# A four-layer graph network on one core: the edge stage of layer 0 keeps its sums in PSUM, with the node's own term copied there by ScalarE

## What is computed

```python
m_in = jnp.concatenate([h[src], h[dst], edge_attr], axis=1)
m = relu(m_in @ eW1 + eb1) @ eW2 + eb2
agg = jax.ops.segment_sum(m, dst, num_segments=h.shape[0])
h_upd = _mlp(jnp.concatenate([h, agg], axis=1), nW1, nb1, nW2, nb2)
return _layer_norm(h + h_upd, ln_gamma, ln_beta)
```

## Time and profile before

| | us |
|---|---|
| median of 3 runs | 4426.26 (4425.43 to 4427.96) |
| the profiled execution | 4430.56 |
| its span in the profile | 4428.8 |
| first addition out of PSUM in the stage begins | 615.7 |
| last accumulation of the stage begins | 1436.4 |

### The profile page before, as it was taken

The page is one execution under the profiler, slowest core; times in us unless marked ns, Lnnn a source line. Parts: engine busy times, 40 slices in busy tenths (PEclk is TensorE's granted clock), DMA queues, the critical chain, the costliest instruction groups (busy, mean ns, idle before and its releaser), DMA issues. The chain is left out here.

```text
span 4428.8 us, 52906 instructions
## 1 busy us (share of the span) xinstructions
PE 2686.6 (61%) x11454; PEld 1433.4 (32%) x11454; DVE 3253.1 (73%) x7572; ACT 719.6 (16%) x2122; POOL 2983.3 (67%) x2929
## 2 busy tenths in 40 slices
PE   4244578888887799466666656578888853000007
PEld 4144332222222688233233334344444422000004
DVE  7497458888888233489999976499989986666664
ACT  0011100000000233233333322111111102000004
POOL 0577667777765577677777737677777745777772
PEclk8555799999999899777888878787888876555558
DMA  3235346666665333466666733376666643444441
GB/s 159 36 113 156 76 123 179 178 178 171 175 173 147 74 62 61 119 173 172 173 172 175 199 67 69 102 186 185 187 186 186 186 112 78 111 108 108 108 106 40
DMA packets 408930, 594.52 MB, mean 134 GB/s; under 512 B 267146, under 2 KB 273430, under 8 KB 407806
## 3 DMA queue, kind: packets, MB, share of 16 engines
q0 software_dynamic: 185552, 519.27, 42.8%
q1 hardware_dynamic: 223278, 74.01, 7.1%
HBM read 532.97 MB, written 59.26 MB: 134 GB/s over the span
## 5 line engine op out<-in xcount | busy, mean ns | idle before, releaser
L1106 POOL DMA_INDIRECT edge_ring<-tab,edge_rec x480 | 475.8, 991 | 146.2 <-issue 135.2
L1688 PE MATMUL edge_psX<-edge_w_edge,edge_featT 64*128 64x256 f32 x1920 | 440.6, 451 | 196.3 <-DVE edge_prod L1764 193.7
L2028 POOL DMA_INDIRECT state<-tab,edge_rec x480 | 453.8, 945 | 155.7 <-issue 145.9
L1693 PE MATMUL edge_psX<-state,ident 128*128 128x512 f32 x720 | 446.2, 753 | 113.9 <-DMA state<-tab,edge_feat 104.2
L1135 PE MATMUL edge_psX<-state,ident 128*128 x720 | 379.6, 637 | 135.3 <-DVE edge_ring L1163 135.3
L1618 POOL DMA_INDIRECT state<-tab,edge_rec x360 | 351.5, 976 | 159.1 <-issue 102.4
L1688 PEld LDWEIGHTS edge_psX<-edge_w_edge,edge_featT 64*128 64x128 f32 x1920 | 297.7, 216 | 465.5 <-issue 401.3
L1618 POOL DMA_INDIRECT state<-tab,edge_feat x360 | 352.0, 978 | 109.7 <-issue 103.9
L2201 PE MATMUL gate_psA<-ident,gate_w_nat 128*128 128x128 f32 x8 | 2.0, 428 | 632.1 <-DMA gate_w_nat<-in_L_gnn_W_ih 632.1
L1163 DVE TENSOR_TENSOR edge_ring<-edge_psX,edge_ring 128x1024 f32<-128x1024 f32 x240 | 293.8, 1224 | 73.3 <-PE edge_psX L1142 43.4
L781 POOL DMA_INDIRECT sorted_d<-update_row_out,update_row_idx x200 | 237.7, 1189 | 92.3 <-issue 59.4
(11 more groups left out here) (439 smaller groups left out, 6362.0 us busy)
## 6 DMA issues: line engine op xcount, KB each, us to landing
sorted_d<-state SPq DMA_DIRECT2D x7, 2380.0 KB
state<-src_rows SPq DMA_DIRECT2D x25, 562.5 KB
state<-low_rows SPq DMA_DIRECT2D x25, 562.5 KB
state<-tab,edge_rec POOLq DMA_INDIRECT x840, 3.0
edge_ring<-tab,edge_rec POOLq DMA_INDIRECT x600, 3.7
update_row_out<-in_edge_attr SPq DMA_DIRECT2D x40, 156.2 KB
edge_rec<-rec_d SPq DMA_DIRECT2D x364, 8.0 KB, 2.8
state<-tab,edge_feat POOLq DMA_INDIRECT x360, 3.7
```

What stands on the lines that cost most here:

```text
L1106: pool.indirect_dma_start(out=ring[:, k, s, :], out_offset=None, in_=S["tab0"][:, :], in_offset=bass.IndirectOffsetOnAxis(ap=rec[:, k, R_S ...
L1688: pe.matmul(psX[k % 2][:, s % 2, s // 2, :], featT[lo:lo + ED, k % 4, s // PAIR, :], w_edge[lo:lo + ED, :], start=(s < 2), stop=False, ski ...
L1693: last = pe.matmul(psX[k % 2][:, a, :, :], S["ident"][:, :], ring[k % RING].rearrange("p (c a) f -> p a c f", a=2)[:, a, :, 0:D], start=Fa ...
L2028: pool.indirect_dma_start(out=ring[:, k, s, :], out_offset=None, in_=S["tab3"][:, :], in_offset=bass.IndirectOffsetOnAxis(ap=rec[:, k, R_S ...
```

## The change

On the side of PSUM:

- Four products at the start of the stage write `psX` once (start flag set). From then on the products add to what stands in `psX`.
- ScalarE reads the quad's block number, and after its copy of the transposed attributes it copies the own term into the four slots of `psX`, each copy raising `own_ready`. Slots 0 and 1 wait for the first `sums_read` of the quad before, slots 2 and 3 for the second.
- TensorE no longer writes the own term. It waits for each slot's copy and adds the attributes' product to it. In slot 0 it also adds the gathered row by a product with the identity, for which it waits for the gathers of rows 0 and 1.
- VectorE adds row 1, and later rows 2 and 3 together, in place in PSUM. It accumulates from PSUM straight into the block's sum in SBUF; `psS` is gone. The ring place is freed after the addition of rows 2 and 3. Slots 0 and 1 are given back after the second accumulation, slots 2 and 3 after the fourth. Own-order waits are placed one by one.

```diff
-        CH = AQ * (QE + 1)
+        CH = AQ * 6
             def _(act):
                 act.nop().then_inc(s_fT, 1)
+                act.wait_ge(s_open, 1)
...
+                        own = blk(S["big2"], block_of(act, t, q))
                         act.wait_ge(s_T, t * AQ + (q + 1))
                         act.activation(featT[:, k % 2, :, :], psT[k % 2][:, 0:2 * P].rearrange("p (c n) -> p c n", c=2), ACT.Copy).then_inc(s_fT, 1)
+                        for s in range(QE):
+                            if s % 2 == 0:
+                                hold(act, s_xr, t * (2 * AQ) + (2 * q + s // 2 + 1))
+                            act.activation(psX[:, s, :], own, ACT.Copy).then_inc(s_own, 1)
...
+                for s in range(QE):
+                    opened = pe.matmul(psX[:, s, :], S["ident"][0:ED, :], w_edge[0:ED, :], start=True, stop=True)
+                opened.then_inc(s_open, 1)
...
-                    b = block_of(pe, t, 0)
...
+                        pe.wait_ge(s_fT, t * AQ + (q + 2))
                         for h in range(2):
-                            pe.wait_ge(s_xr, t * (2 * AQ) + (2 * q + h + 1))
-                            for i in range(2 - h):
-                                pe.matmul(psX[:, 2 * h + i, :], S["ident"][:, :], blk(S["big2"], b), start=True, stop=False)
...
+                            for i in range(2):
+                                lo, s = ED * i, 2 * h + i
+                                pe.wait_ge(s_own, t * (QE * AQ) + (QE * q + 2 * h + 1 + i))
+                                last = pe.matmul(psX[:, s, :], featT[lo:lo + ED, k % 2, h, :], w_edge[lo:lo + ED, :],
+                                                 start=False, stop=(s > 0), skip_group_check=True)
                             if h == 0:
+                                pe.wait_ge(s_g[k][0], uses(t, q, RING_0) * 32)
+                                last = pe.matmul(psX[:, 0, :], S["ident"][:, :], ring[:, k, 0, :], start=False, stop=True, skip_group_check=True)
                             last.then_inc(s_x, 1)
...
+                        acc = blk(S["big"], b)
+                        hold(dve, s_g[k][0], uses(t, q, RING_0) * 32)
+                        dve.wait_ge(s_x, t * (2 * AQ) + (2 * q + 1))
+                        row1 = step.put(dve.tensor_tensor(psX[:, 1, :], psX[:, 1, :], ring[:, k, 1, :], ALU.add))
+                        first = step.put(dve.scalar_tensor_tensor(acc, psX[:, 0, :], 0.0, acc, ALU.max, ALU.add))
+                        hold(dve, s_g[k][1], uses(t, q, RING_0) * 32)
+                        dve.wait_ge(s_x, t * (2 * AQ) + (2 * q + 2))
+                        rows23 = step.put(dve.tensor_tensor(psX[:, 2:4, :], psX[:, 2:4, :], ring[:, k, 2:4, :], ALU.add))
+                        if q < AQ - 1:
+                            b_next = block_of(dve, t, q + 1)
+                        step.until(first)
+                        second = step.put(dve.scalar_tensor_tensor(acc, psX[:, 1, :], 0.0, acc, ALU.max, ALU.add))
+                        step.until(rows23)
                         dve.nop().then_inc(s_done[k], 1)
+                        step.until(second)
+                        dve.nop().then_inc(s_xr, 1)
+                        step(dve.scalar_tensor_tensor(acc, psX[:, 2, :], 0.0, acc, ALU.max, ALU.add))
+                        step(dve.scalar_tensor_tensor(acc, psX[:, 3, :], 0.0, acc, ALU.max, ALU.add))
+                        dve.nop().then_inc(s_xr, 1)
```

More of the change, by code:

```diff
@@ L1069, in edge_mlp @@
         psX = ph.ps("psX", [P, QE, D2])
-        psS = ph.ps("psS", [P, D2])
         s_rec, s_done, s_feat = ([ph.sem(f"{n}{k}") for k in range(RING_0)] for n in ("rec_loaded", "quad_done", "feat_loaded"))
         s_g = [[ph.sem(f"rows{k}_{h}") for h in range(2)] for k in range(RING_0)]
-        s_w, s_v, s_T, s_fT, s_x, s_xr = (ph.sem(n) for n in (
-            "weights_loaded", "dve_step", "feat_turned", "featT_ready", "sums_ready", "sums_read"))
+        s_w, s_v, s_T, s_fT, s_x, s_xr, s_open, s_own = (ph.sem(n) for n in (
+            "weights_loaded", "dve_step", "feat_turned", "featT_ready", "sums_ready", "sums_read", "sums_open", "own_ready"))
         turns = lambda eng: eng.value_load(S["turns0"][0:1, 0:1], min_val=1, max_val=NG_PAD // AQ)
-        CH = AQ * (QE + 1)
+        CH = AQ * 6
         def block_of(eng, t, q):
@@ L1131, in _ @@
                         pe.transpose(psT[k % 2][:, P:2 * P], feat[:, k, P:2 * P], S["ident"][:, :]).then_inc(s_T, 1)
+                        pe.wait_ge(s_fT, t * AQ + (q + 2))
                         for h in range(2):
-                            pe.wait_ge(s_xr, t * (2 * AQ) + (2 * q + h + 1))
-                            for i in range(2 - h):
-                                pe.matmul(psX[:, 2 * h + i, :], S["ident"][:, :], blk(S["big2"], b), start=True, stop=False)
-                            if h and q < AQ - 1:
-                                b = block_of(pe, t, q + 1)
-                            if h == 0:
[L1139 to L1143, removed]
+                            for i in range(2):
[3 more added lines that the diff above has]
+                                                 start=False, stop=(s > 0), skip_group_check=True)
+                            if h == 0:
+                                pe.wait_ge(s_g[k][0], uses(t, q, RING_0) * 32)
+                                last = pe.matmul(psX[:, 0, :], S["ident"][:, :], ring[:, k, 0, :], start=False, stop=True, skip_group_check=True)
                             last.then_inc(s_x, 1)
@@ L1156, in _ @@
                         k, b = q % RING_0, b_next
[L1157 to L1170, removed]
```

## The result

The changed kernel takes 4697.52 us (median of 4 runs, 4696.03 to 4699.17), the kernel before 4427.11 beside it: a ratio of 1.061, interval 1.0592 to 1.0628. The forecast of "slower" was right, its size was not: +121 us were forecast, +270 measured, above the range's upper end of 4650. The nearest rival was C (4673), to which I gave 0.10 and which my range left out.

What follows compares the result with a forecast made beforehand. VectorE was taken to bound the edge stage before, the PSUM slot ring after: 6.80 us plus 1.05 for the clock, 7.85 per quad over 120 quads, +121 us, giving 4547 us; range 4415 to 4650.

Steps and rivals of the forecast that it cites:

- C: Rival: clock low nearly all the time, slots 2 and 3 late too; 8.9 us per quad, 4673 us; chance 0.10.
- The ring: Layer 0's edge stage: refilling PSUM slots through ScalarE, TensorE and VectorE sums to 6.80 us per quad at full clock.
- second accumulation to ScalarE: Handing slots 0 and 1 back, from VectorE's second accumulation to ScalarE's first copy: 0.20 us, between 0.1 and 0.3.
- VectorE to the second accumulation: VectorE's row 1 addition, first accumulation, addition of rows 2 and 3, and second accumulation: 3.15 us per quad.
- What is hidden: Edge-stage work claimed off the critical path: late accumulations, turn pauses, gathers, opening products; slots 2 and 3 have 0.3 us spare.
- The four opening products lie before the first gather has landed: At the edge stage's start, TensorE's products that first write PSUM were claimed hidden, adding nothing to the time.
- The clock: TensorE's gap of some 2.5 us drops its clock in about 4 of 5 quads, adding 1.05 us per quad.
- everything at 1.2 GHz: Upper bound on the clock's cost per quad: 2.1 us on slot 1 and row 0, 0.8 on slots 2 and 3.
- signs named: Expected in the new trace's edge stage: waits, gaps, copy times, VectorE busy share, granted clock and quads of 7.3 to 8.4 us.
- B: Rival: TensorE's clock holds at 2.4 GHz in the edge stage; 4421 us, or 4385 with short terms; chance 0.20.
- D: Rival: VectorE instructions reading PSUM cost 62 cycles more, adding 31 us, 4578 us; chance 0.05.
- E: Rival: VectorE relieved, rows freed early, gathers bind at 6.36 us per quad, 4368 us; chance 0.03.

Runs made afterwards that it cites:

- e1: Changed kernel plus two unused identity products per quad on TensorE, between its transposes and its wait for the own term: 4408.51 us, ratio 0.9955 to the kernel before.
- e3: Changed kernel with two PSUM buffers for slots 0 and 1, filled by ScalarE before its copy of the transposed attributes: 4357.68 us, ratio 0.9842 to the kernel before.
- e15: Changed kernel with TensorE waiting for both own copies of a pair before the pair's first product, on an undisturbed chip: 4549.78 us, ratio 1.0272 to the kernel before.
- e14: Changed kernel plus one unused identity product per quad on TensorE, on an undisturbed chip: 4523.67 us, ratio 1.0224 to the kernel before.
- e4: ScalarE's own-term copies alone: VectorE as in the kernel before without its own-term addition, slots handed back by the 1024-column additions: 4375.44 us, ratio 0.9883.
- e13: The changed kernel itself, unedited, measured again on an undisturbed chip: 4695.23 us, ratio 1.0609 to the kernel before.
- e16: Changed kernel plus four unused half-array products of 64 rows per quad on TensorE, on an undisturbed chip: 4405.81 us, ratio 0.9948 to the kernel before.
- e5: Changed kernel plus one unused identity product per quad, on a chip with stalls where the kernel before took 5340.98 us: ratio 0.9944.

## Why the prediction was wrong in size

**The ring: right.** e1 shows it at full clock:

| term | forecast | e1 |
|---|---|---|
| second accumulation to ScalarE | 0.20 | 0.23 (1008.40 to 1008.63) |
| two copies | 1.09 | 1.12 |
| handover and slot 1's product | 0.09 + 1.06 | 1.11 (1009.75 to 1010.86) |
| row 0's product, handover to VectorE | 1.13 + 0.08 | 1.12 + 0.04 |
| VectorE to the second accumulation | 3.15 | 3.02 (1005.38 to 1008.40) |
| quad | 6.80 | 6.64 |

The forecast's -5 us over the stage for the sum at full clock is -18 us in e1 (4408.51 against 4426.96). All five terms lie within 0.13. The weight load of slot 1 was not hidden either: in e1 it starts at 1009.80, 0.05 after ScalarE's second copy.

**What is hidden: right at full clock only.** VectorE's waits met, no turn's pause, gathers not late: all as forecast in e1. One item was wrong at any clock: "The four opening products lie before the first gather has landed". That gather is issued at 608.29, and in the kernel before the first transpose starts 2.95 us after the issue; by this estimate it had landed at 611.24. The products ended at 613.43. They are part of the 4.9 us at the stage's start, which the sum put at nothing. At 1.2 GHz the 0.3 us of spare time on slots 2 and 3 is gone: rows 2 and 3 waited 71.6 us over 115 quads, 0.62 each:

```profile
DVE edge_psX L1165 <- PE edge_psX L1148: 433.7, 115, 4.0
...
DVE edge_psX L1169 <- PE edge_psX L1144: 71.6, 115, 0.7
```

**The clock: the step that failed.** It read "I expect a fall in about 4 of 5 quads" and "0.8 x 1.3 = 1.05". Measured: 9.08 - 6.64 = 2.44 us a quad. Slot 1's product and row 0's, from the copies' end to the end, take 4.12 us (1016.91 to 1021.03) where e1 has 2.23 (1009.75 to 1011.98), +1.89; the wait at rows 2 and 3 adds about 0.6. Both halves of the term were too small: row 0's product ran at half clock in 120 quads of 120, not in 4 of 5, and the price was 2.44, not 1.3. I took the rate of falls from the attention stage (mean clock 0.78) and from the earlier trace rows, where the clock was back within the same refill, before its last products (those of slot 2 and of the pair at 676.75 and 677.81 took 1.13 us each). Here it stayed low across a gap and most of the next quad's work. Stretches of one microsecond in the changed kernel (TensorE busy, granted clock, DMA, GB/s):

```profile
1003.00:1004.00 1.00, 1.00 (x4) 0.50 0.22 86
...
1006.00:1007.00 1.00, 0.00 (x0) 0.50 0.80 221
...
1010.00:1011.00 1.00, 1.00 (x3) 0.50 0.00 0
...
1013.00:1014.00 1.00, 1.00 (x6) 0.90 0.75 221
1014.00:1015.00 1.00, 0.06 (x1) 1.00 0.68 209
1015.00:1016.00 1.00, 0.00 (x0) 1.00 0.74 164
1016.00:1017.00 1.00, 0.56 (x2) 0.81 0.78 201
1017.00:1018.00 1.00, 1.00 (x4) 0.50 0.49 159
```

Where the clock does come back, from 1013 on, TensorE has only its transposes left (0.33 and 0.27 there, 0.47 and 0.42 a quad earlier) and then idles; it falls in the microsecond in which the next products start (1016.44). The full clock is granted mostly to the gap: read in stretches of 0.25 us from 700 to 1400, it holds for 181 us, and TensorE is idle in 121 of them. My bound "everything at 1.2 GHz" (2.1 + 0.8 = 2.9) held, and rival C's 8.9 us a quad was nearly the truth (9.08). I argued against C that TensorE would then be busy nearly without a gap, and that the stages' means say the clock comes back. It does come back, but into the gap. And the first was wrong: VectorE's 3 us and ScalarE's copies stand in the ring whatever the clock, so a gap of over 2 us remains at 1.2 GHz as well.

Of the signs named, row 1's wait (1.5 or more: 3.95), TensorE's gap (2 or more: 2.1 to 2.4) and the own copies (near 0.60: 0.592) came. VectorE at 60 to 65% busy (49%), a clock of 0.75 to 0.9 (0.62 to 0.64) and quads of 7.3 to 8.4 us (9.08) did not; all three hang on the clock.

**The rivals.** B (clock holds) is what e1 produced by force, 4408.51 against its 4421. D (PSUM reads slower): the accumulations from PSUM take 0.680 to 0.692, no more than the 0.70 of the one that reads SBUF alone, and the 512-column addition takes 0.700 with PSUM as a source where L1161 in the kernel before took 0.69 from SBUF alone. So the trace disagrees here too with the 62 cycles (0.065 us, an estimate) of the Trainium skill (VectorE: DVE Perf Modes, "The TRN2 errata"). E needs a second buffer: e3, 4357.68, below its 4368.

## What to carry to other kernels

When a buffer passes through three engines and is handed back late, add up the ring at both levels of TensorE's clock. Where the ring itself leaves TensorE idle each time round, give the low level a full place in the forecast: here idle times of 2.1 to 2.4 us went with 1.2 GHz in the ring's products in every quad, 3.0 us in 37 of 120 (e15), 1.7 us in 53 of 120 (e14), 0.8 us in none (e1). Why the clock stayed low in every quad was not found, so carry the two sums over, not the rate. A second buffer for the slots on the ring gave the shortest time here (e3), and a few products of no use (e1) show in one run whether the clock is the cause. Hand PSUM back at the first read where that can be had: e4 lost nothing at a clock of 0.57 to 0.60.

## What the runs showed of the hardware

- With the same products per quad, the granted clock was 0.62 with the pair of half-array products 0.5 us apart and 0.83 with the two at once after a longer wait (e13, e15).
- A ScalarE copy of 512 columns from SBUF into PSUM takes 0.592 us, two in a row 1.12.
- Fillers of 64 rows in both halves of the array held the clock at 1.00 as the full ones did (e16, e1).
- A gather issued by GpSimd took 0.945 us while VectorE added in place in PSUM (e3) and 0.989 in the kernel before, where VectorE writes its sums to SBUF. The cause was not tested.
- On two chips the kernel before took 5341 and 5434 us instead of 4427. In the traces from there single engines are idle for 10 us and more (in e5, VectorE for 10.22 us before 1225.71). The cause was not looked for.
